# A three-part decoder layer in one pipelined loop: attention denominators by ln, exp and one Newton step, two small jobs moved to GpSimd, and a new order of steps

## The reference, cut to what matters

```python
# stage a: causal linear attention, 16 heads of 16
q, k = elu(q) + 1, elu(k) + 1
den = scores.sum(-1) + einsum('bhcd,bhd->bhc', q_c, z)
y   = num / (den[..., None] + 1e-06)
x   = x + y @ w_proj.T
# stage b: cross attention on tanh probabilities against ctx, then a GELU MLP and a layernorm
sid  = einsum('bnd,bmd->bnm', q_prob - k_prob, log(q_prob) - log(k_prob))
attn = softmax(-sid / D ** 0.5)
x    = x + layernorm(mlp(layernorm(f_diff)) + f_diff)
# stage c: a router picks 128 of the 256 tokens; these go through softmax attention and a SiLU MLP
scores = x @ w_router;  _, idx = top_k(scores, 128)
out    = x.at[idx].set(x_sel + x_attn + x_ff)
```

## Time and profile before

| | |
|---|---|
| time, median of 3 runs | 884.62 us (884.0 to 886.33) |
| the profiled execution's own time | 886.46 us |
| its span | 884.6 us, 21235 instructions |
| busy in the span | PE 811.2 (92%), PEld 700.4, DVE 723.9 (82%), ACT 559.0 (63%), POOL 274.8 (31%) |
| TensorE clock granted, mean | 0.986 |
| rounds in the steady part | one per 49.7 us |

### The profile page before, as it was taken

One profiled execution on the slowest core, in us unless ns is written; L12 is line 12 of the kernel. 1 busy time (PEld: TensorE's weight loads), 2 busy tenths in 40 slices (PEclk: granted clock), 3 DMA queues, 4 the chain that ended last, 5 costly groups with the idle time before them and its releaser, 6 DMA issues.

```text
span 884.6 us, 21235 instructions
## 1 busy us (share of the span) xinstructions
PE 811.2 (92%) x7219; PEld 700.4 (79%) x7219; DVE 723.9 (82%) x1689; ACT 559.0 (63%) x1517; POOL 274.8 (31%) x443
## 2 busy tenths in 40 slices
...
DMA packets 31223, 44.02 MB, mean 50 GB/s; under 512 B 2512, under 2 KB 23120, under 8 KB 31184
## 3 DMA queue, kind: packets, MB, share of 16 engines
...
...
## 4 chain that ended last, share of the span: by engine, by line
PE 58%; DVE 16%; ACT 14%; issue 8%; POOL 2%; DMA 1%; DVEq 0%; ACTq 0%; SPq 0%; POOLq 0%
PE bank L1134 14%; ACT w_raw_or_stage_c L723 9%; PE bank L1238 4%; PE bank L1256 4%; PE bank L1318 4%; PE bank L1393 3%; PE bank L1512 3%; PE bank L1326 3%; PE bank L1142 3%; PE bank L1296 3%; PE bank L1150 3%; ACT L723 2%; PE bank L1418 2%; DVE prob L918 2%; PE bank L1438 2%
## 5 line engine op out<-in xcount | busy, mean ns | idle before, releaser
L678 ACT ACTIVATE prob<-bank,b_folded 128x256 f32<-128x256 f32 x128 | 53.7, 470 | 100.0 <-PE bank L1134 99.8
L873 DVE TENSOR_TENSOR a_s<-bank,const 128x512 f32<-128x512 f32 x112 | 72.6, 685 | 46.9 <-PE bank L1238 25.2
L723 ACT ACTIVATE w_raw_or_stage_c<-bank,c_nmax 128x128 f32<-128x128 f32 x256 | 90.0, 402 | 3.2 <-DVE c_nmax L1047 3.0
L539 POOL DMA_INDIRECT out<-w_raw_or_stage_c,row_of_slot_out x16 | 17.3, 1080 | 181.5 <-DVE w_raw_or_stage_c L1101 181.5
L723 ACT ACTIVATION_READ_ACCUMULATOR w_raw_or_stage_c<-bank,c_nmax 128x1 f32 x256 | 62.0, 242 | 0.0
L790 DVE TENSOR_TENSOR b_s_lo<-prob,b_s_hi 128x512 fp32r<-128x512 f32 x64 | 43.2, 675 | 20.9 <-ACT b_s_hi L564 20.9
L1429 PE MATMUL bank<-const,w_raw_or_stage_c 128*128 128x128 f32 x256 | 40.3, 280 | 16.5 <-ACT w_raw_or_stage_c L723 16.5
L863 DVE RECIPROCAL a_e<-a_e 128x512 f32<-128x512 f32 x16 | 53.5, 3344 | 0.0
L1429 PEld LDWEIGHTS bank<-const,w_raw_or_stage_c 128*128 128x128 f32 x256 | 28.1, 141 | 26.0 <-ACT w_raw_or_stage_c L723 16.9
L1047 DVE TENSOR_REDUCE c_nmax<-bank 128x4 f32<-128x512 f32 x64 | 41.8, 677 | 8.0 <-PE bank L1418 8.0
L1134 PE MATMUL bank<-b_s_hi,w_mlp_hi 128*128 128x256 f32 x256 | 45.2, 299 | 2.4 <-ACT prob L678 1.4
(11 more groups left out here) (256 smaller groups left out, 2699.1 us busy)
## 6 DMA issues: line engine op xcount, KB each, us to landing
...
x_in<-in_x SPq DMA_DIRECT2D x16, 256.0 KB, 3.4
qc<-in_ctx SPq DMA_DIRECT2D x16, 256.0 KB, 2.7
b_f<-in_ctx_t SPq DMA_DIRECT2D x16, 256.0 KB, 2.9
x<-in_x SPq DMA_DIRECT2D x16, 256.0 KB, 2.7
out<-w_raw_or_stage_c SPq DMA_DIRECT2D x16, 256.0 KB, 2.2
...
```

What stands on the lines that cost most here:

```text
L678: act_in(prob[:, 2 * (j % 2) + n, :], b0[:, n * T:(n + 1) * T], ACT.Gelu, bias=b1p[:, f:f + 1]).then_inc(b_gelu.sem, 1)
L723: act_in(c_e[g % 2][:, j * R:(j + 1) * R], C_SCORES[g][:, j * R:(j + 1) * R], ACT.Exp, bias=c_nmax[:, n:n + 1], accum_out=c_den[:, head:he ...
L873: tt(heads(A_MASKED[t][n][:, :]), heads(A_SCORES[n][:, :]), tri.unsqueeze(1).broadcast_to([P, 4, P]), ALU.mult).then_inc(a_scput.sem, 1)
```

## The change

Four things change.

1. `a_dinv`'s reciprocal goes. `a_dput` becomes two ACT instructions, r = exp(-ln(den + 1e-6)). A new DVE step `a_dnear` computes near = (den + 1e-6) * r from a0, and `a_dinv` computes (near - 2) * r, one Newton step with its sign turned. `a_y` multiplies by -1 besides. `a_score_0` now waits for `a_dnear`, the last reader of a0, where it waited for `a_dput`.
2. `c_ob` becomes one POOL addition of 128x512 and loses its helper `c_obs`. `c_keep` moves from DVE to POOL.
3. The POOL additions of an epsilon become additions of a constant tile (TENSOR_TENSOR in place of TENSOR_SCALAR).
4. ORDER, WEIGHTS_AT and WARM_AT are new. The counts of WARM_AT add up to 146 where they were 69.

```diff
             def a_dput_(b):
                 act_e.wait_ge(*a_den(b))
-                act_in(a_e1[:, :], a0[:, :], ACT.Identity, bias=C["den_eps"]).then_inc(a_dput.sem, 1)
+                act_in(a_e1[:, :], a0[:, :], ACT.Ln, bias=C["den_eps"]).then_inc(a_dput.sem, 1)
+                act_e.wait_ge(*a_dput(b, 1))
+                act_in(a_e1[:, :], a_e1[:, :], ACT.Exp, scale=-1.0).then_inc(a_dput.sem, 1)
...
+            def a_dnear_(b):
+                dve.wait_ge(*a_dput(b))
+                stt(a_near, a0[:, :], DEN_EPS, a_e1[:, :], ALU.add, ALU.mult).then_inc(a_dnear.sem, 1)
+
             def a_dinv_(b):
-                dve.wait_ge(*a_dput(b))
-                nc.vector.reciprocal(a_e1[:, :], a_e1[:, :]).then_inc(a_dinv.sem, 1)
+                dve.wait_ge(*a_dnear(b))
+                stt(a_e1[:, :], a_near, 2.0, a_e1[:, :], ALU.subtract, ALU.mult).then_inc(a_dinv.sem, 1)
...
-                tt(flat(a_norm[:, :, :]), a0[:, :], a_e1[:, :], ALU.mult).then_inc(a_y.sem, 1)
+                stt(flat(a_norm[:, :, :]), a0[:, :], -1.0, a_e1[:, :], ALU.mult, ALU.mult).then_inc(a_y.sem, 1)
...
                     if t == 0:
                         pe.wait_ge(*a_mask(b))
-                        pe.wait_ge(*a_dput(b))
+                        pe.wait_ge(*a_dnear(b))
...
-            def power(b, source, in_, eps, out_, done):
+            def power(b, source, in_, out_, done):
...
-                nc.gpsimd.tensor_scalar(out_, in_, eps, None, ALU.add).then_inc(done.sem, 1)
+                nc.gpsimd.tensor_tensor(out_, in_, C["ln_eps"], ALU.add).then_inc(done.sem, 1)
...
+            def c_ob_(b):
+                pool.wait_ge(*c_normed(b))
+                if not first(b):
+                    pool.wait_ge(*out_done(b - 1))
+                nc.gpsimd.tensor_tensor(ob[:, :, :], x2[:, :, :], c_norm[:, :, :], ALU.add).then_inc(c_ob.sem, 1)
+
+            def c_keep_(b):
+                pool.wait_ge(*c_idxput(b))
+                if not first(b):
+                    pool.wait_ge(*y_stored(b - 1))
+                    pool.wait_ge(*c_next(b - 1))
...
+                nc.gpsimd.tensor_scalar(index_out[:, :], index[:, :], batch_at[:, 0:1], None, ALU.add).then_inc(c_kept.sem, 1)
...
-            def c_ob_(b):
-                act_e.wait_ge(*c_obs(b))
...
-                    act_in(ob[:, t, :], x2[:, t, :], ACT.Identity, bias=c_offset[:, t:t + 1], scale=c_gain[:, t:t + 1]) \
...
-c_w2 b_frstd+ c_gthi_0++ c_gtlo_0++ c_ob+ b_fput+ b_fmean+ c_gthi_1++ a_kput+ a_sput+ b_fd+ c_gtlo_1++ c_hsc+
...
+c_gthi_0++ a_kput+ c_ff_0++ c_gthi_1++ a_state+ a_dinv+ a_rstd+ c_ff_1++ b_hlo+ a_scput_0+ c_ht+ b_htp+
```

More of the change, by code:

```diff
@@ L44 @@
 ORDER = """
-c_w2 b_frstd+ c_gthi_0++ c_gtlo_0++ c_ob+ b_fput+ b_fmean+ c_gthi_1++ a_kput+ a_sput+ b_fd+ c_gtlo_1++ c_hsc+
-a_mask+ c_ff_0++ a_state+ b_fnormed+ a_den+ c_w6 a_dput+ c_ff_1++ a_scput_0+ a_scput_1+ b_hlo+ a_scput_2+
-a_scput_3+ c_w8 c_ht+ a_score_0+ c_hput+ b_htp+ a_mean b_hhi+ a_scput_4+ c_qkput+ c_qk+ b_up_0+ c_w4
-a_score_1+ a_scput_5+ a_scput_6+ b_gelu_0+ c_v+ a_att_0+ b_up_1+ a_scput_7+ a_att_1+ b_down_0+ c_w1 c_vput+
-b_ghi_0+ b_glo_0+ b_up_2+ c_score+ b_gelu_1+ c_y++ b_up_3+ c_put++ b_ghi_1+ a_dinv+ c_w7 b_glo_1+ b_gelu_2+
@@ L55 @@
-c_mean a_tlo c_idx c_h2put+ c_h2hi+ b_pnorm c_gu_1+ c_h2lo+ a_qout b_log c_normed b_diff c_rscore b_vq b_dtp
-c_tanh_0+ c_rank a_kout c_sel c_tanh_1+ b_rtp b_ratio b_kept c_idxput b_dput c_gu_2+ b_sid b_fb2 a_phi_q
-b_rput c_gate_0+ a_phi_k c_gtp_0+ a_vput c_gate_1+ a_csum c_gtp_1+ a_kq a_ktp b_sexp
+a_kout+ c_gu_1++ b_dtp+ b_rtp+ c_tanh_1++ c_gu_2++ b_sid+ b_fput+ b_dput+ b_rput+ b_fmean+ a_ktp+ c_gtlo_1++
+c_gtp_0++ c_gtp_1++ a_vput+ b_kept++ a_sput+ b_fd+ a_den+ c_hsc+ b_fnormed+ a_mask+ b_sexp+ a_dnear+ c_y++
```

80 lines of the change are left out of this document (33 added, 47 removed).

## The result

The kernel after takes 872.9 us (median of 4 runs, 871.53 to 876.35) against 884.65 for the kernel before in the same job: ratio 0.987, with a 95% interval of 0.984 to 0.990. The forecast was 880.0 with a range of 869 to 892. The time lies in the range, but the gain is 11.8 us where the sum had 4.3, and it does not lie where the forecast put it.

What follows compares the result with a forecast made beforehand. PE and DVE were taken as both nearly full, PE setting S1 and DVE S2. From 884.6, 13 rounds at -0.14 gave -1.8 and the ends -2.5: 880.3 us (the result says 880.0, range 869 to 892).

Steps and rivals of the forecast that it cites:

- S1: Round from b_sid to the end of c_score, where PE sets the pace; to grow from 24.34 to 26.42 us.
- S2: Round from c_score's end to c_sel's end, where DVE runs full; to fall from 22.41 to 20.00 us.
- S3: Round from c_sel's end to the next b_sid; PE's part to stay unchanged at 2.89 us.
- ACT and POOL, 0.09 and 0.10: Additions per round: ACT's way to b_sid 0.09 us later than PE's, POOL's late c_rms_half delaying the tanh load 0.10.
- POOL late: Rival: c_h2rms on POOL comes the full 0.8 us late; +0.56 a round, 889.4 us; chance 0.15.
- signs of being right: Round 49.3 to 49.7, PE waiting 0.4 at b_htp, no DVE gap over 0.6 in S2, two loads without PE wait.
- signs of being wrong: Tanh load over 0.5 late, a_st waiting for x_in with late maxima, or PE waiting for a_dnear at a_score_0.
- SP late: Rival: c_ob on POOL delays SP's store and next x; beyond slack about 1, 13 us per us; 893; chance 0.13.
- More gain: Rival: the 0.45 and 0.10 don't arise, DVE gets ahead; 0.7 us less a round, 873 us; chance 0.17.
- Nothing moves: Rival: another wait in PE takes the 0.14 us gained per round; 884 us; chance 0.07.
- Table loads with a drain: Rival: ACT table switches cost a drain too, so Exp's path to a_score_0 lengthens; +1.8 a round, 904 us; chance 0.03.
- Start and end: Outside the 13 rounds: -1.5 us from stage a in rows 0 and 1, -1.0 from clock matmuls; together -2.5.

Runs made afterwards that it cites:

- run 10: The kernel after with the old reciprocal back as two instructions of 256 elements, placed where DVE waits for PE; ratio 0.984 to the kernel before.
- run 7: The kernel after with the table set holding both ln and exp loaded by name, one load in place of two; ratio 0.989 to the kernel before.
- Run 12: The kernel after with POOL's order c_put, c_ob, b_kept, c_keep and the loop's cut moved right behind a_dput; 862.8 us, ratio 0.973 to the kernel before.
- run 9: The kernel after with POOL's steps in the order c_put, c_ob, b_kept, c_keep; ratio 0.985 to the kernel before.
- runs 1 and 2: All clock-keeping matmuls removed, from the kernel after in 1 (ratio 1.000 to the kernel before) and from the kernel before in 2 (1.007).
- runs 3 and 11: 3: the kernel after, five round-2 weight splits moved to round 1, ratio 0.995. 11: the kernel before, last five splits one round later, 1.000.
- Run 8: The kernel after with the old denominators, the whole reciprocal back at a_dinv's place; ratio 1.004 to the kernel before.

## Why the prediction was right or wrong

The forecast took `b_sid` from the chain (397.75), and the timeline, from which all that follows is read, has it at 397.67. With that mark its three stretches are 26.50, 20.00 and 2.81.

**S1, `b_sid` to the end of `c_score`:** 26.50 forecast, 26.26 measured. PE shows no wait at the `b_htp` transposes; `b_htp` and `a_score_0` are done 10.29 after `b_sid`, 0.28 later than before, where I had 0.45. Cost 0 for Ln and Exp was right: S1 is 26.26 in run 10 too, which has neither, and run 7 without the second load changed nothing. The loads show no drain: the second one starts 0.02 after Ln, ends at 398.72, and Exp starts at 398.74. The 2.66 per switch of the Trainium skill's page "ScalarE: Activation LUTs", section "What ACT_TABLE_LOAD costs", is not what this kernel pays; its 1283 ns agrees.

**S2, to the end of `c_sel`:** 20.00 forecast, 20.41 measured (`c_sel` ends at 437.82). The terms for work moved out were right. The wait ahead of the maxima did not fall to 0.10 but is 0.39 of DVE's own lateness, +0.3, and the rank trip is 0.67 for 0.50.

**S3, to the next `b_sid`:** 2.81 forecast, 3.35 measured. "PE's part is unchanged" is a step that failed: the table was cut inside S3, and the jump was not in my sum. From `c_idx` to `c_gu_1` it is 0.61 for 0.06, and the rest of S3 is as before. Run 12 has 2.77 from `c_idx` to `b_sid` where after has 3.29.

**ACT and POOL, 0.09 and 0.10:** neither came. `c_rms_half` ends at 435.43, before `b_log` does (436.09). L491, the old L494, takes 0.20 beside the one-input scalings where it took 1.31; that it would lose most of that was in the forecast. The rival *POOL late* is out.

**A round** was thus 50.02 and not 49.50. Taking the late x away gave 0.3 (run 9) and moving the cut as well another 0.5 (run 12); against these stand the 0.24 of S1 and the 0.19 of ACT and POOL that did not come. Of my signs of being right, the round of 49.3 to 49.7 and the wait at `b_htp` failed and the two loads without a PE wait held; of my signs of being wrong, one came: `a_st` waits for `x_in`, and the maxima start late.

**The rival *SP late*** named the right chain, with its times nearly right (`a_mean` at 21.2 for "near 21"), and the wrong threshold. I had said that `a_mean` could start as late as 22.3. But the DVE steps from it to the maxima take 5.45 (412.35 to 417.80) and not 4.1, one of them 1.59 instead of 0.69 beside POOL's 1.29 us `b_fb2`. So it decides from 20.8, and costs 0.3 to 0.4 a round. The forecast had nothing for it in the sum.

**The other rivals.** *More gain* gave 873, the time that came, but by a round 0.7 shorter; the round became longer, so its mechanism is out. *Nothing moves* is out with the ends, and *Table loads with a drain* with the rows of ACT.

**Start and end** is the term that was mis-sized: -2.5, open from -8 to +4, and it measured -17.9 in the profiles, outside its own bounds. The size of the gain came from here. The term's own working had a fault besides: it charged rows 0 and 1 with a table load of 1.28, and they have none, and it left out the Newton step of 0.68. What the runs settle: some 5 us of the whole is the new clock matmuls (runs 1 and 2), some 5 the later splits, and only in the new order (runs 3 and 11). Run 8 is 1.4 to 4.0 later at the third `b_sid` than the kernels with the shorter denominators, and 1.1 of that is what each of its rounds loses. These parts overlap and do not make a sum. In the drain 7.9 of 8.1 stands without clock matmuls, part of it with a higher clock. One part can be read: SP's store of the token rows, from which the tokens are picked. Before:

```profile
839.74 0.36 SPq L395 DMA_DIRECT2D token_rows<-norm_x_rms  x1
```

After:

```profile
829.70 0.36 SPq L393 DMA_DIRECT2D token_rows<-norm_x_rms  x1
```

Before, it stands 0.46 ahead of `c_idx` (840.20), and the picked rows are used 7.77 after `c_idx`; after, it stands 2.52 ahead (832.22), and they are used at 5.76. That is 2.0 us, from `c_rms1` on POOL standing ahead of `c_h2rms`. Another 1.9 lies behind the last `c_put`: it starts 6.0 to 6.1 before the end of the span in runs 2 and 11, as in before, and 4.1 to 4.2 in every kernel with the order of after. What that is, and the other 4 us of the drain, stays open; the clock may hold some of the latter.

So the time was forecast within 1%, by a sum whose loop term had the wrong sign (-1.8 for +4.2) and whose end terms were too small by 15. That the two errors stood against each other, and the time came to lie in the range, was luck.
